# Last layer of a fused kernel: token weights spread over the lanes by DMA and multiplied onto the input, eight experts accumulated in PSUM; an earlier store, and one product for each column sum

## What is computed

```python
def _L3_ffn_ref(x, gate_weight, experts):        # x: the normalised tokens, experts: (8, 128, 128)
    gate_logits = jnp.einsum('bhnd,hde->bhne', xh, gate_weight)
    gates = _sinkhorn(gate_logits)               # 8 rounds: over the tokens, then over the experts
    g_t = jnp.swapaxes(gates, -1, -2)
    vals, idx = jax.lax.top_k(g_t, m)            # each expert takes the m = n / 8 tokens of largest gate
    ...
    outputs = jnp.einsum('ebhmi,ehio->ebhmo', routed, expert_w)
    outputs = outputs * gate_values
    ...                                          # scattered back; of several experts on one token the last stays
x = _from_tokens(t + _L3_ffn_ref(_ln_t(t), ...), x)
```

## Time and profile before

| | |
|---|---|
| median of 3 runs (lowest to highest) | 4431.47 us (4424.26 to 4435.53) |
| the profiled execution, its time | 4427.38 us |
| its span | 4425.6 us |
| TensorE busy / its weight loads | 3569.1 us (81%) / 2263.7 us (51%) |
| VectorE busy | 3069.9 us (69%) |
| ScalarE busy | 1871.3 us (42%) |
| GpSimd busy | 1101.2 us (25%) |
| mean granted TensorE clock | 0.883 |

### The profile page before, as it was taken

The page is one execution under the profiler, slowest core; times in us unless marked ns, Lnnn a source line. Parts: engine busy times, 40 slices in busy tenths (PEclk is TensorE's granted clock), DMA queues, the critical chain, the costliest instruction groups (busy, mean ns, idle before and its releaser), DMA issues. The chain is left out here.

```text
span 4425.6 us, 133748 instructions
## 1 busy us (share of the span) xinstructions
PE 3569.1 (81%) x55247; PEld 2263.7 (51%) x55247; DVE 3069.9 (69%) x7658; ACT 1871.3 (42%) x4391; POOL 1101.2 (25%) x1955
## 2 busy tenths in 40 slices
PE   5999999997698406776468999998689999985398
PEld 1222222222366403443347788876377888765276
DVE  7777777764766522333678999997789999973643
ACT  1655656663344002223346655553366655542000
POOL 1000000000000572332026553332165443320000
PEclk6999999998799558998559999998599999995599
DMA  6022232200000211113100000000000000001000
GB/s 132 16 36 49 50 50 50 50 7 6 1 1 15 81 50 39 50 47 92 67 7 9 14 9 9 9 5 6 6 10 9 14 9 6 6 10 42 0 0 38
DMA packets 89311, 122.12 MB, mean 28 GB/s; under 512 B 16020, under 2 KB 59929, under 8 KB 88432
## 3 DMA queue, kind: packets, MB, share of 16 engines
q1 hardware_dynamic: 75632, 90.65, 8.5%
q0 software_dynamic: 13088, 23.06, 1.8%
HBM read 69.65 MB, written 45.04 MB: 26 GB/s over the span
## 5 line engine op out<-in xcount | busy, mean ns | idle before, releaser
L2055 ACT ACTIVATE s_E<-s_Y,s_M 128x9 f32<-128x9 f32 (+38 forms) x2048 | 656.5, 392 | 627.3 <-DVE s_M L1968 625.0
L343 DVE TENSOR_REDUCE half_max<-bm 128x1 f32<-128x512 f32 x1024 | 652.9, 685 | 221.8 <-PE bm L264 217.8
L1869 PE MATMUL g_x<-s_ik,s_iqm 128*32 128x1 f32 (+63 forms) x16384 | 673.5, 280 | 26.4 <-DVE g_o L1951 11.6
L455 ACT ACTIVATE E<-sc 128x1024 f32<-128x1024 f32 x512 | 521.3, 1025 | 349.5 <-PE sc L278 338.5
L1963 DVE SCALAR_TENSOR_TENSOR s_Y<-s_Y,g_x 128x9 f32<-128x9 f32 (+38 forms) x2048 | 578.1, 282 | 47.3 <-PE g_x L1869 1.4
L1881 PE MATMUL g_p<-mats,s_E 128*128 128x128 f32 x3072 | 449.1, 283 | 42.4 <-ACT s_E L2055 38.8
L264 PE MATMUL bm<-ks,qs 96*128 96x512 bf16 x1024 | 413.7, 406 | 73.4 <-DVE half_max L343 42.2
L1869 PEld LDWEIGHTS g_x<-s_ik,s_iqm 128*32 128x32 f32 x16384 | 392.1, 116 | 152.2 <-issue 75.4
L1881 PEld LDWEIGHTS g_p<-mats,s_E 128*128 128x128 f32 x3072 | 339.6, 144 | 110.1 <-ACT s_E L2055 66.3
L264 PEld LDWEIGHTS bm<-ks,qs 96*128 96x128 bf16 x1024 | 99.0, 97 | 545.5 <-DVE half_max L343 458.6
L1968 DVE TENSOR_REDUCE s_M<-s_Y 128x4 f32<-128x8 f32 (+56 forms) x512 | 351.0, 686 | 0.3
(11 more groups left out here) (352 smaller groups left out, 5455.1 us busy)
## 6 DMA issues: line engine op xcount, KB each, us to landing
d_parts<-parts SPq DMA_DIRECT2D x8, 1536.0 KB, 5.9
qs<-d_parts SPq DMA_DIRECT2D x96, 128.0 KB, 8.4
ks<-d_parts SPq DMA_DIRECT2D x96, 128.0 KB, 11.6
me_xg<-d_xs SPq DMA_DIRECT2D x144, 65.0 KB, 1.8
mc_yb<-d_ys SPq DMA_DIRECT2D x8, 1024.0 KB
resid<-in_x SPq DMA_DIRECT2D x8, 512.0 KB, 8.3
rden<-d_den POOLq DMA_DIRECT2D x16, 256.0 KB, 3.7
m_w_gu<-in_gate_up SPq DMA_DIRECT2D x1, 4096.0 KB, 12.3
```

Of the source, the lines that this page charges most:

```text
L343: dve.tensor_reduce(half_max[n // SETS % 2][:, idx // 2, idx % 2:idx % 2 + 1], bm[n % 2][:, :], AX_X, ALU.max).then_inc(max_done, 1)
L455: act.activation(E[:, G % 2, h, :], sc[n % 2][:, :], ACT.Exp, scale=0.25).then_inc(exp_done, 1)
L1869: mm = pe.matmul(x_ps[u % 3][32 * b:32 * (b + 1), rho % 2, 0:n + 1], iqm[n // WINDOW % 2][:, b, x0:x0 + D, :], s.ik[:, b, rho, 0:n + 1], s ...
L2055: act.activation(E[:, m % 2, rho, 0:m + 1], Y[:, D * (m % YR) + rho, 1:2 + m], ACT.Exp, bias=M[:, D - 1 + D * m + rho:D + D * m + rho]).th ...
```

## The change

In `sinkhorn_gates` VectorE first adds the eight tiles of `gate` (a reduction over j, read with a step of 64 elements) into `part` [128, 64], and TensorE forms the column sums with one product of `part` in place of eight.

`routed_experts` is written anew, without loops, over 64 pairs k of sample b and expert e. The weights `f.weight` are turned (eight transposes of [128, 64]) into PSUM as 64 rows of 1024 tokens; ScalarE copies these to `rows` in SBUF, and SyncE writes them to a DRAM tensor `d_gate` (256 KB). Once that has landed, SyncE reads row k of it onto all 128 lanes (`spread`, 512 KB, six buffers), VectorE multiplies it onto the sample's input (`xw`, 1024 columns, three buffers), and TensorE multiplies expert e, as the stationary matrix, with it: two products of 512 columns, accumulated over the eight experts in `z_ps` [128, 1024]. The output has channels on the lanes at once. VectorE adds a whole sample to `t.resid` behind the third scaling of the next sample, and ScalarE issues the store of each sample as soon as it is added. `store_result` and the GpSimd copies go.

```diff
                 for n in range(SINKHORN):
-                    pe.wait_ge(step, n + 1)
-                    for j in range(NT):
-                        mm_ = pe.matmul(c_ps[:, 0:B, :], ones[:, :], gate[:, j, :, :], start=j == 0, stop=j == NT - 1)
-                    mm_.then_inc(colsum, 1)
+                    pe.wait_ge(tiles_added, n + 1)
+                    pe.matmul(c_ps[:, 0:B, :], ones[:, :], part[:, :, :], start=True, stop=True).then_inc(colsum, 1)
...
                 for n in range(SINKHORN):
+                    dve.wait_ge(step, n + 1)
+                    dve.tensor_reduce(part[:, :, :], gate[:, :, :, :].rearrange("p j b e -> p b e j"), AX_X, ALU.add
+                                      ).then_inc(tiles_added, 1)
                     dve.wait_ge(colsum, n + 1)
...
-                    dve.wait_ge(step, n + 2)
...
+def routed_experts(nc, t, f, out, d_gate):
+
+    RING = 6
+    PAIRS = B * NEX
...
+            @block.sync
+            def _(sp):
+                sp.wait_ge(taken, 1)
+                sp.dma_start(d_gate, rows[:, :]).then_inc(sent, 16)
+                sp.wait_ge(sent, 16)
+                for k in range(PAIRS):
+                    if k >= RING:
+                        sp.wait_ge(scaled, k - RING + 1)
+                    sp.dma_start(spread[k % RING][:, :], d_gate[k:k + 1, :].to_broadcast([P, T])).then_inc(w_in[k % RING], 16)
+
+            @block.scalar
+            def _(act):
+                act.wait_ge(turned, 1)
+                act.activation(rows[:, :], w_ps[:, :], ACT.Copy).then_inc(taken, 1)
+                for b in range(B):
+                    act.wait_ge(added, b + 1)
+                    act.dma_start(out[b], t.resid[:, b * T:(b + 1) * T]).then_inc(stored, 16)
+                act.wait_ge(stored, 16 * B)
...
+                for j in range(NT):
+                    tr = pe.transpose(w_ps[:, j * P:(j + 1) * P], f.weight[:, j, :, :], t.mat("ident"))
+                tr.then_inc(turned, 1)
+                for k in range(PAIRS):
+                    b, e = k // NEX, k % NEX
+                    pe.wait_ge(scaled, k + 1)
+                    if e == 0 and b >= 2:
+                        pe.wait_ge(added, b - 1)
+                    for h in range(2):
+                        mm_ = pe.matmul(z_ps[b % 2][:, h * HALF:(h + 1) * HALF], f.experts[:, e, :],
+                                        xw[k % 3][:, h * HALF:(h + 1) * HALF], start=e == 0, stop=e == NEX - 1)
+                    mm_.then_inc(mm, 1)
...
+                def add(b):
+                    dve.wait_ge(mm, NEX * (b + 1))
+                    r = t.resid[:, b * T:(b + 1) * T]
+                    dve.tensor_tensor(r, z_ps[b % 2][:, :], r, ALU.add).then_inc(added, 1)
+
+                for k in range(PAIRS):
+                    b, e = k // NEX, k % NEX
+                    dve.wait_ge(w_in[k % RING], 16 * (k // RING + 1))
+                    if k >= 3:
+                        dve.wait_ge(mm, k - 2)
+                    dve.tensor_tensor(xw[k % 3][:, :], t.xn[:, b * T:(b + 1) * T], spread[k % RING][:, :], ALU.mult
+                                      ).then_inc(scaled, 1)
+                    if e == 2 and b:
+                        add(b - 1)
+                add(B - 1)
```

More of the change, by code:

```diff
@@ L2233, in sinkhorn_gates @@
         rcol = sb("rcol", [P, B, NEX])
+        part = sb("part", [P, B, NEX])
         rsum = sb("rsum", [P, NT, B])
@@ L2248, in sinkhorn_gates @@
         g_ps = ctx.enter_context(nc.psum_tensor("k_g", [BE, T], F32))
-        loaded, const, mm, step, colsum, turned, picked, chain, back = (
-            sem("loaded"), sem("const"), sem("mm"), sem("step"), sem("colsum"), sem("turned"), sem("picked"), sem("chain"), sem("back"))
+        loaded, const, mm, step, colsum, turned, picked, chain, back, tiles_added = (
+            sem("loaded"), sem("const"), sem("mm"), sem("step"), sem("colsum"), sem("turned"), sem("picked"), sem("chain"), sem("back"),
+            sem("tiles_added"))
         with nc.Block() as block:
@@ L2367, in routed_experts @@
         ctx.callback(sem.give_back)
[L2368 to L2373, removed]
-        with nc.Block() as block:
[L2375 to L2381, removed]
+        rows = sb("rows", [PAIRS, T])
@@ new lines, in routed_experts @@
+        spread = [sb(f"spread{i}", [P, T]) for i in range(RING)]
+        xw = [sb(f"xw{i}", [P, T]) for i in range(3)]
+        w_ps = psum("w", [PAIRS, T])
+        z_ps = [psum(f"z{i}", [P, T]) for i in range(2)]
+        turned, taken, sent = sem("turned"), sem("taken"), sem("sent")
+        w_in = [sem(f"w_in{i}") for i in range(RING)]
+        scaled, mm, added, stored = sem("scaled"), sem("mm"), sem("added"), sem("stored")
+        with nc.Block() as block:
+            @block.sync
[15 more added lines that the diff above has]
+                act.wait_ge(stored, 16 * B)
@@ L2383, in _ @@
             @block.tensor
             def _(pe):
[L2385 to L2410, removed]
@@ L2448, in layer3_ffn @@
         sinkhorn_gates(nc, t, f)
[L2449 to L2458, removed]
+        routed_experts(nc, t, f, out, d_gate)
 class Tensors:
@@ L2491, in build @@
     d_ys = nc.dram_tensor("d_ys", (2 * N, P), F32, kind="Internal").ap()
+    d_gate = nc.dram_tensor("d_gate", (B * NEX, T), F32, kind="Internal").ap()
     d_resid = nc.dram_tensor("d_resid", (P, N), F32, kind="Internal").ap()
@@ L2507, in build @@
         token_norm(nc, t, "n5", "eps5")
-        layer3_ffn(nc, t, io)
-        store_result(nc, t, out)
+        layer3_ffn(nc, t, io, out, d_gate)
 def constants():
```

3 lines of the change are left out of this document (1 added, 2 removed).

## The result

| | before | changed |
|---|---|---|
| median (lowest to highest) | 4432.33 us (4424.26 to 4435.53), 4 runs | 4300.08 us (4297.84 to 4304.88), 4 runs |
| profiled execution | 4427.38 us | 4304.88 us |
| its span | 4425.6 us | 4303.2 us |
| from the first use of the gates to the end | 358.0 us | 227.7 us |

The account below looks back on a forecast made before the run. TensorE was taken to bound the expert loop. 114.4 us saved in loop, start and end plus 16.0 in column sums, 130.4 off 4427.4, gave 4297.0, with 4.1 to the median 4301; 8 in 10 range 4286 to 4368.

Parts of the forecast that it names:

- a column sum's stretch: Sinkhorn rounds, last multiplication to reciprocal: 1.85 us instead of 3.85, saving 16.0 us over eight rounds.
- the products: Expert loop on TensorE: 64 pairs at 1.72 us, 110.1 us, plus 2.2 us for the lower starting clock, 112.3.
- last product to the end: End of the kernel: last add, one store, handovers and semaphore clearing take 5.1 us instead of 13.6.
- saved in loop and store: Expert loop with its start and end: finishes at 4311.2 instead of 4425.6, 114.4 us less.
- The bound: Expert loop: TensorE bounds before and after; VectorE and DMA, each 11.5 us of a sample's 13.8, fit under it.
- The start: Before the expert loop's first product: transposes, copy, write to DRAM, load and scaling, uncovered, make it 9.4 us later.
- The one row that no trace showed: Expert loop's load of one 4 KB row onto 128 lanes: 1.28 us taken, 2.66 at rden's 197 GB/s.
- the slower rival: Expert loop: every load runs at 135 GB/s, 3.88 us each, total 4446 us, slower than before; chance 4%.
- The Trainium skill's rule against small transfers: Expert loop's 512 KB transfers: 1.54 us each at 341 GB/s, 13.8 us a sample, level with TensorE; not used.
- The stepped read: Column sum's reduction over 512 columns: 0.69 us contiguous plus 0.33 for the step, 1.02 us.
- The clock: Rival in the expert loop: TensorE's clock stays at 0.50, loop 220 us, total 4409; chance 3%.
- the marks to look for: Signs in the later profile, such as loop clock 1.00, products 1.72 us apart, loads some 340 GB/s, share 0.8 to 0.9.

Follow-up runs that it names:

- e1: The kernel before with the column sums alone changed (reduction over eight tiles, one product); 0.9969 of the time before, last stretch 341.7 us against 358.0.
- e2: The changed kernel with the eight products per column sum put back, so only expert loop and store changed; 0.9734 of the time before, last stretch 243.8 us.
- e4: The changed kernel with half the tokens' columns left out of the expert loop's work, all loads and stores kept; 0.9645 of the time before.
- e5: As e4, but every load reads 128 different 4 KB rows of the kernel's input instead of one row 128 times; 0.9639 of the time before.
- e6: The changed kernel with two buffers for the spread weights in place of six; 4379 us, 0.9879 of the time before.
- e9: The changed kernel with four buffers for the spread weights in place of six; last stretch 232.9 us against the changed kernel's 227.7.
- e3: The changed kernel with all eight stores issued after the last add; 0.974 of the time before, last stretch 236.9 us against 227.7.

## Why the prediction was right, point by point

| term | forecast, us | measured, us |
|---|---|---|
| a column sum's stretch | 1.85 | 1.83 |
| the reduction in it | 1.02 | 1.01 |
| saved in eight rounds | 16.0 | 16.3 (e1) |
| weights done to first product | 11.7 | 12.0 |
| the products | 112.3 | 112.2 |
| last product to the end | 5.1 | 5.1 |
| saved in loop and store | 114.4 | 114.2 (e2) |

- *The bound* stayed where it was put: TensorE at clock 1.00 without a gap. The turns of the earlier trace rows went and the projections stayed in the shape of the new products, at the same price; the table's 112.2 is from 4185.88 to 4298.1, with the first microseconds at the lower clock in it.
- *The start* came out right as a sum, with its terms off both ways: the block change took 0.8 us to the transposes in place of 1.1, the write to DRAM with the next issue 2.9 in place of 2.4, the first load 4.0 in place of 3.6 and a handover. Both transfers were priced from 256 KB ones.
- *The one row that no trace showed*, 128 reads of one row, was taken at 1.28 us from the earlier trace rows and from the share in the earlier trace rows. e4 measured 1.28, and e5 the same with rows of its own. Reading GB/s by the share of engines that were busy was what decided it: the 197 GB/s of rden over 0.48 are 410. That step came out well by luck. The same division gives 340 / 0.95 = 358 for the changed kernel's loop and 191 / 0.57 = 335 for e6's, though the same engines move 420 when DMA paces (e4). What the price really rests on is the earlier trace rows, full engines, and e4's full engines agree. The 135 GB/s of the earlier trace rows, from which the slower rival came, belong to another shape, as was argued; no run here shows why that shape is slow.
- *The Trainium skill's rule against small transfers* (DMA: Bandwidth & Descriptors, Bandwidth, Measured: at least 1 MiB, 341 GB/s for 1 MB, measured there on transfers that GpSimd issued) doesn't hold here: 512 KB transfers issued by SyncE, one behind the other, moved 420 GB/s in e4.
- *The stepped read.* (1011 - 686) / 512 is 0.63 ns more a column, as the stepped writes of the earlier trace rows had it. The Trainium skill (Vector Engine (DVE) Microarchitecture Reference, the SBUF access granule) gives 1.73 ns a column for one source that hops 4 KiB at every element, against 1.054 for contiguous ones. That is 0.68 more, and the trace's 0.63 is near it. Its 2.50 is for steps of 24 words on both sources or on the destination, and it has no price for one source with a step of 64, as here.
- *The clock* was not the loop's trouble: it read 1.00 from 4190 on, and e6 kept 1.00 with TensorE busy two thirds of the time, but for the start and one stretch of 3.4 us.
- *What was wrong* stood among the marks to look for: the DMA share was to be 0.8 to 0.9 and was 0.95, and a load was to take 3.6 us to land and took 6.1. That touched no term, since six buffers cover 10.3 us. It is right by that margin and not by its reading: with four buffers the same latency would have promised no wait (4 x 1.72 = 6.9 us), and e9 lost 5.2 us.
- *Luck.* That the median came within 1 us of 4301 is chance: the four runs of the kernel before spread over 11 us, and its median moved by some 30 us between groups of runs. What the prediction can claim is the last stretch, 130.3 us shorter for 130.4, and its terms in the table.

## What to carry to other kernels

Price a new product by a product of the same shape that is already in the trace, and everything that feeds it by its own time per turn of the loop; when all of them fit under the bound, the sum stands. Put a weight on the side where it needs no turn afterwards: here scaling the input made eight transposing products per tile unnecessary, 114 us of the engine that bounds, for some 34 MB of DMA traffic that otherwise idle engines carried. Choose the number of buffers by the time from issue to landing under the loop's own load, not by that of a lone transfer, and look for what runs uncovered ahead of the loop: there an edit pays in full.

## What the runs showed that I had not expected

- The share of busy DMA engines isn't a measure of what they have left. The loop showed 0.95 at 340 GB/s and 0.88 to 0.92 at 306 (e3, without stores), yet the same engines moved 420 GB/s at 1.03 (e4) when they paced. The room is found by letting DMA pace, not from the share. Windows of e3:

```profile
4200.00:4230.00 30.00, 30.00 (x72) 13.28 (x71) 24.11 (x21) 0.00 (x0) 0.00 (x0) 1.00 0.92 306
4230.00:4260.00 30.00, 30.00 (x72) 13.27 (x71) 23.62 (x21) 0.00 (x0) 0.00 (x0) 1.00 0.88 305
```

- From issue to landing a 512 KB load took 4.7 us (median) with two in flight at 200 GB/s, 5.8 with four at 320, 6.1 with six at 340, and 8.0 when DMA paced (e4).
- The layers ahead of the change scatter more between chips and executions than most edits here are worth: with the same program ahead, the last stretch began at 4059.3 us (e3) to 4105.6 us (e1).
